# Gating expert results per block and scatter-adding them into an output that already holds the residual rows

## What is computed

```
x  = x + attention(layer_norm(x)) @ Wo + bo
nx = layer_norm(x)
noisy = nx@Wr + br + noise * softplus(nx@Wn + bn)
the two highest of the 8 experts are kept, softmax over the two
out = x                                where sigmoid(nx@Wsk + bsk) > 0.5
out = x + sum over the two e of gate_e * (relu(nx@W1[e] + b1[e]) @ W2[e] + b2[e])   elsewhere
```

## Time and profile before

| | us |
|---|---|
| median of three runs | 861.09 |
| span of the profiled execution, first to last instruction | 859.4 |
| first stage and table, to the first second-stage matmul | about 530 |
| second stage, to the landing of the last scatter | about 238 |
| third stage | about 91.5 |

### The profile page before, as it was taken

One profiled execution on the slowest core, in us unless ns is written; L12 is line 12 of the kernel. 1 busy time (PEld: TensorE's weight loads), 2 busy tenths in 40 slices (PEclk: granted clock), 3 DMA queues, 4 the chain that ended last, 5 costly groups with the idle time before them and its releaser, 6 DMA issues.

```text
span 859.4 us, 32083 instructions
## 1 busy us (share of the span) xinstructions
PE 591.5 (69%) x11076; PEld 428.8 (50%) x11076; DVE 651.0 (76%) x2422; ACT 482.6 (56%) x947; POOL 483.5 (56%) x540
## 2 busy tenths in 40 slices
PE   0668787777778888877776512999999999820000
PEld 0336565555555555555554411777777777610000
DVE  2367888989888888899897571787778877618887
ACT  1547666575756576666665421888888888600000
POOL 3113777777777677777777673266666666530000
PEclk9889799999998789999998555999999999955555
DMA  9862231322213132313435336666777666329997
GB/s 93 253 182 82 59 91 57 90 64 84 87 58 91 52 86 60 92 54 91 105 82 162 101 109 214 255 226 222 238 241 247 224 226 237 117 76 301 292 298 224
DMA packets 164172, 127.32 MB, mean 148 GB/s; under 512 B 38050, under 2 KB 142595, under 8 KB 164128
## 3 DMA queue, kind: packets, MB, share of 16 engines
q1 hardware_dynamic: 127264, 90.00, 35.8%
q10 hardware_dynamic: 24576, 20.98, 8.3%
q0 software_dynamic: 12288, 15.77, 5.6%
HBM read 73.86 MB, written 62.78 MB: 159 GB/s over the span
## 4 chain that ended last, share of the span: by engine, by line
PE 33%; DVE 19%; issue 16%; ACT 14%; DMA 8%; POOL 3%; ACTq 3%; DVEq 2%; SPq 1%; POOLq 0%
DMA out<-z 6%; ACT z L666 5%; PE ps L500 5%; DVE stats L816 4%; PE ps L628 3%; PE ps L616 3%; PE ps L534 3%; PE ps L629 3%; PE ps L630 3%; PE ps L617 3%; PE ps L618 3%; POOL expert_rows L1123 3%; PE ps L537 2%; PE ps L546 2%; ACT hT L695 2%
## 5 line engine op out<-in xcount | busy, mean ns | idle before, releaser
L1123 POOL DMA_INDIRECT expert_rows<-pay,rows_of x256 | 256.7, 1003 | 103.0 <-issue 70.0
L1136 POOL DMA_INDIRECT expert_results<-z,words x128 | 134.5, 1051 | 107.6 <-DVE z L1007 76.3
L1021 DVE TENSOR_TENSOR hlo<-h,hhi 128x512 fp32r<-128x512 f32 x128 | 89.8, 702 | 45.6 <-ACT hhi L773 43.8
L771 ACT ACTIVATE h<-ps,w1x 128x512 f32<-128x512 f32 x128 | 88.2, 689 | 35.2 <-PE ps L618 31.5
L666 ACT ACTIVATE z<-xres,shift,rstd 128x128 f32 (+1 forms) x256 | 102.0, 481 | 2.5 <-DVE shift L848 2.5
L773 ACT ACTIVATE hhi<-ps,w1x 128x512 fp32r<-128x512 f32 x128 | 87.1, 681 | 0.0
L534 PE MATMUL ps<-hT,wq 128*128 128x512 f32 x64 | 47.9, 839 | 55.5 <-ACT hT L695 55.5
L682 ACT ACTIVATE log_var<-var_eps 128x8 f32<-128x8 f32 (+1 forms) x36 | 7.5, 208 | 130.3 <-DVE var_eps L830 110.7
L1104 POOL TENSOR_TENSOR xres<-xres,bo_row 128x512 f32 (+1 forms) x32 | 41.6, 1299 | 55.8 <-ACT z L666 55.5
L546 PEld LDWEIGHTS ps<-pT,v_sb 32*32 32x32 f32 x4096 | 47.6, 106 | 49.0 <-issue 46.8
L546 PE MATMUL ps<-pT,v_sb 32*32 32x32 f32 x4096 | 58.1, 204 | 11.3 <-issue 4.2
(11 more groups left out here) (138 smaller groups left out, 1454.4 us busy)
## 6 DMA issues: line engine op xcount, KB each, us to landing
w1x<-split_weights SPq DMA_DIRECT2D x33, 514.0 KB, 3.7
w2x<-split_weights SPq DMA_DIRECT2D x33, 512.5 KB, 5.0
expert_results<-zeros SPq DMA_DIRECT2D x32, 512.0 KB, 4.1
pay<-expert_rows SPq DMA_DIRECT2D x33, 264.0 KB, 3.5
xres<-in_r_x SPq DMA_DIRECT2D x32, 256.0 KB, 3.1
split_weights<-w2x ACTq DMA_DIRECT2D x16, 512.0 KB
hhi<-expert_results SPq DMA_DIRECT2D x32, 256.0 KB, 3.8
hlo<-expert_results SPq DMA_DIRECT2D x32, 256.0 KB, 3.7
```

What stands on the lines that cost most here:

```text
L771: nc.scalar.activation(h32[:, c % 2], ps[:, c, :], ACT.Relu, bias=b1_c).then_inc(s_h32_made, 1)
L1021: ev.tensor_tensor(hlo[:, c], h32[:, c % 2], hhi[:, c].bitcast(F32), ALU.subtract).then_inc(s_h_lo, 1)
L1123: g.indirect_dma_start(rows, bass.IndirectOffsetOnAxis(ap=rows_of[:, odd, k * J + j:k * J + j + 1], axis=0), pay[:, odd, k, j, :], None, b ...
L1136: g.indirect_dma_start(results, bass.IndirectOffsetOnAxis(ap=words[:, slot, j:j + 1], axis=0), yrow[slot][:, j, :], None, bounds_check=K * ...
```

## The change

- The output tensor gets 512 spare rows behind the 16384 real ones; the host cuts them off. The result table, its zeroing and the whole third stage are gone.
- In the first stage SP stores the finished residual rows x1 of the tile six before the one it loads, 256 KB each (`store_x1`), in the place of zeroing. The last six stores come after the loop and the biases, ahead of the wait for the fill counts. A blank tile is stored to the spare rows.
- `gdiff` is no longer kept. Two DVE instructions write, in columns 129 and 130 of `pay`, the difference v1-v0 for both choices, and v1-v0 or 0 for the numerator. They travel with the row. The wait for the earlier scatter of `pay` comes before them.
- The word is the token's number, the same for both choices. Blank rows have words that point into the spare rows, so that they are written there and no longer dropped.
- In each block ACT makes one `Exp` of the two columns (`gate_rows`), DVE three small instructions (`make_gates`: add one, reciprocal, multiply), and `copy_rows` multiplies by the gate on the way out of PSUM. It also waits for the gate.
- The scatter adds into the output (`compute_op=ALU.add`). Since two blocks can hold the same token, the scatter of a block first waits until all four DMAs of the block before have landed.

The diff, cut to its core (left out: the declarations of buffers and semaphores, and lines that don't change):

```diff
--- before.py
+++ after.py
@@ -53,15 +53,14 @@
+    BEHIND = 4
...
-    out_t = out.rearrange("b t c -> (b t) c").rearrange("(n p) c -> p n c", p=P)
+    out_t = out[0:N, :].rearrange("(n p) c -> p n c", p=P)
...
-    results = nc.dram_tensor("expert_results", [K * N, C], F32, kind="Internal").ap()
-    results_t = results.rearrange("(k n p) c -> p k n c", k=K, p=P)
@@ -187,11 +179,10 @@
-        yin = [hhi[:, 0:K], hhi[:, K:2 * K], hlo[:, 0:K], hlo[:, K:2 * K]]
-        yin = [y.rearrange("p k (j c) -> p k j c", c=C).bitcast(F32) for y in yin]
-        half = z1
-        fin = z2
+        gate_e = sb("gate_e", [P, 4, J, 2])
+        gate_d = sb("gate_d", [P, J])
+        gate_r = sb("gate_r", [P, J])
+        gate = sb("gate", [P, 4, J])
@@ -399,10 +382,10 @@
-            def zero_results(n):
...
-                sp.dma_start(results[bass.ds(n * K * G, K * G), :].rearrange("(p r) c -> p r c", p=P),
-                             zeros[:].unsqueeze(1).to_broadcast([P, K * J, C])).then_inc(s_results_zeroed, 16)
+            def store_x1(n):
...
+                sp.wait_ge(s_x1_made, n + 1)
+                sp.dma_start(out_t[:, bass.ds(n * J, J), :], tiles(xres, n)).then_inc(s_x1_out, 16)
@@ -423,14 +406,13 @@
-            sp.wait_ge(s_zeros_set, 1)
-            with sp.Fori(2, NG - 1, 2) as n:
+            for n in range(2, BEHIND + 2):
+                load_x(n, n % 2)
+            with sp.Fori(BEHIND + 2, NG - 1, 2) as n:
...
-                zero_results(n)
+                store_x1(n - BEHIND - 2)
...
-                zero_results(n + 1)
-            zero_results(0)
-            zero_results(1)
+                store_x1(n - BEHIND - 1)
@@ -449,6 +431,10 @@
+            sp.dma_start(out[N:N + G, :].rearrange("(p j) c -> p j c", j=J),
+                         blank[:, :, 0:C]).then_inc(s_x1_out, 16)
+            for n in range(NG - BEHIND - 2, NG):
+                store_x1(n)
@@ -468,7 +454,8 @@
-                          (s_words_kept, i - 3))
+                          (s_words_kept, i - 3),
+                          (s_gate_exp, i - 3))
@@ -479,18 +466,8 @@
+            apart(sp, (w1_in[0], used * 4 + 16), (w2_in[0], used * 4 + 16))
...
-            def load_results(n, slot):
-                apart(sp, (s_f_made, n - 3))
-                for k in range(K):
-                    sp.dma_start(yin[slot][:, k], results_t[:, k, bass.ds(n * J, J), :]).then_inc(f_in[slot], 16)
...
-            for n in range(4):
-                load_results(n, n)
-            with sp.Fori(4, NG - 3, 4) as n:
-                for d in range(4):
-                    load_results(n + d, d)
@@ -753,9 +730,10 @@
-            act.wait_ge(s_route, NG * ROUTE)
-            nc.scalar.activation(gexp[:], gdiff[:], ACT.Exp).then_inc(s_gate_exp, 1)
...
+            def gate_rows(i, slot):
+                act.wait_ge(e_in[slot], quad(i, slot, 16) + 16)
+                wait(act, s_gate, i - 3)
+                nc.scalar.activation(gate_e[:, slot], xg[slot][:, :, C + 1:C + 3], ACT.Exp).then_inc(s_gate_exp, 1)
@@ -773,20 +751,13 @@
+                    if c == 2:
+                        gate_rows(i + 1, (slot + 1) % 4)
...
+            gate_rows(0, 0)
...
-            def store(n, par):
-                act.wait_ge(s_f_made, n + 1)
-                act.dma_start(out_t[:, bass.ds(n * J, J), :], fin[:, par]).then_inc(f_out[par], 16)
...
-            with nc.scalar.Fori(0, NG - 1, 2) as n:
-                store(n, 0)
-                store(n + 1, 1)
-            for q in f_out:
-                act.wait_ge(q, 16 * NG // 2)
@@ -878,8 +849,11 @@
-                    ev.tensor_tensor(gdiff[:, bass.ds(n * J, J)], top[:, :, 1], top[:, :, 0],
-                                     ALU.subtract).then_inc(s_route, 1)
+                    wait(dve, sent[odd], pair(n, odd, SENT))
+                    second = top[:, :, 1].unsqueeze(1).to_broadcast([P, K, J])
+                    first = top[:, :, 0].unsqueeze(1).to_broadcast([P, K, J])
+                    ev.tensor_tensor(pay[:, odd, 1, :, C + 2], top[:, :, 1], top[:, :, 0], ALU.subtract)
+                    ev.tensor_tensor(pay[:, odd, :, :, C + 1], second, first, ALU.subtract).then_inc(s_route, 1)
@@ -934,6 +908,7 @@
+            dve.wait_ge(s_pay_zeroed, 1)
@@ -976,18 +951,6 @@
-            dve.wait_ge(s_gate_exp, 1)
-            ev.tensor_scalar(gden[:], gexp[:], 1.0, None, ALU.add).then_inc(s_gate, 1)
-            dve.wait_ge(s_gate, 1)
-            ev.reciprocal(gfirst[:], gden[:]).then_inc(s_gate, 1)
-            dve.wait_ge(s_gate, 2)
-            ev.tensor_tensor(gates[:, :, 0], gfirst[:], keep[:], ALU.mult).then_inc(s_gate, 1)
-            ev.tensor_tensor(gsecond[:], gexp[:], gfirst[:], ALU.mult).then_inc(s_gate, 1)
-            dve.wait_ge(s_gate, 4)
-            ev.tensor_tensor(gates[:, :, 1], gsecond[:], keep[:], ALU.mult).then_inc(s_gate, 1)
-            dve.wait_ge(s_gate, 5)
@@ -1004,12 +967,23 @@
-                ev.tensor_copy(yrow[slot].rearrange("p j c -> p (j c)"), ps[:, 6, :]).then_inc(s_yrow_copied, 1)
+                dve.wait_ge(s_gate, i + 1)
+                ev.tensor_tensor(yrow[slot], ps[:, 6, :].rearrange("p (j c) -> p j c", c=C),
+                                 gate[:, slot].unsqueeze(2).to_broadcast([P, J, C]),
+                                 ALU.mult).then_inc(s_yrow_copied, 1)
...
+            def make_gates(i, slot):
+                dve.wait_ge(s_gate_exp, i + 1)
+                ev.tensor_scalar(gate_d[:], gate_e[:, slot, :, 0], 1.0, None, ALU.add).then_inc(s_gate_den, 1)
+                dve.wait_ge(s_gate_den, i + 1)
+                ev.reciprocal(gate_r[:], gate_d[:]).then_inc(s_gate_inv, 1)
+                dve.wait_ge(s_gate_inv, i + 1)
+                ev.tensor_tensor(gate[:, slot], gate_r[:], gate_e[:, slot, :, 1], ALU.mult).then_inc(s_gate, 1)
@@ -1024,34 +998,16 @@
+                make_gates(i + 1, (slot + 1) % 4)
...
+            make_gates(0, 0)
...
-            def combine(n, slot):
-                par = slot % 2
-                dve.wait_ge(f_in[slot], quad(n, slot, 16 * K) + 16 * K)
-                for j in range(J):
-                    m = ev.scalar_tensor_tensor(half[:, par, j:j + 1], yin[slot][:, 0, j:j + 1],
-                                                tile(gates, n, j)[:, 0, 0:1], tile(xres, n, j), ALU.mult, ALU.add)
-                m.then_inc(s_f_half, 1)
-                dve.wait_ge(s_f_half, n + 1)
-                wait(dve, f_out[par], pair(n, par, 16))
-                for j in range(J):
-                    m = ev.scalar_tensor_tensor(fin[:, par, j:j + 1], yin[slot][:, 1, j:j + 1],
-                                                tile(gates, n, j)[:, 0, 1:2], half[:, par, j:j + 1], ALU.mult, ALU.add)
-                m.then_inc(s_f_made, 1)
...
-            for n in range(4):
-                combine(n, n)
-            with nc.vector.Fori(4, NG - 3, 4) as n:
-                for d in range(4):
-                    combine(n + d, d)
@@ -1089,12 +1044,12 @@
-            g.iota(token[:], [[N, K], [P, J]], base=0, channel_multiplier=1,
+            g.iota(token[:], [[0, K], [P, J]], base=0, channel_multiplier=1,
...
-            g.iota(blank_u[:, :, C:C + 1], [[0, J]], base=FAR, channel_multiplier=0).then_inc(s_blank_word, 1)
+            g.iota(blank_u[:, :, C:C + 1], [[1, J]], base=N, channel_multiplier=J).then_inc(s_blank_word, 1)
@@ -1132,17 +1087,19 @@
+                if has(i - 1):
+                    apart(pool, (res_out[(slot - 1) % 4], quad(i - 1, (slot - 1) % 4, 16 * J) + 16 * J))
...
-                    g.indirect_dma_start(results, bass.IndirectOffsetOnAxis(
+                    g.indirect_dma_start(out, bass.IndirectOffsetOnAxis(
...
-                        yrow[slot][:, j, :], None, bounds_check=K * N - 1,
-                        oob_is_err=False).then_inc(res_out[slot], 16)
+                        yrow[slot][:, j, :], None, bounds_check=N + G - 1,
+                        compute_op=ALU.add).then_inc(res_out[slot], 16)
...
-            pool.wait_ge(s_results_zeroed, 16 * NG)
+            pool.wait_ge(s_x1_out, 16 * (NG + 1))
@@ -1165,7 +1122,9 @@
-    out = nc.dram_tensor("out_0", inputs['r_x'].shape, _mybir.dt.float32, kind="ExternalOutput").ap()
+    shape = inputs['r_x'].shape
+    rows = shape[0] * shape[1]
+    out = nc.dram_tensor("out_0", (rows + 512, shape[2]), _mybir.dt.float32, kind="ExternalOutput").ap()
...
-    return r.results[0]["out_0"]
+    return r.results[0]["out_0"][:rows].reshape(shape)

```

More of the change, by code:

```diff
@@ L80, in build @@
         ones = sb("ones", [P, P], BF16)
-        zeros = sb("zeros", [P, P])
         filler = sb("filler", [P, 2 * P], BF16)
@@ L98, in build @@
         noise_sb = sb("noise_sb", [P, N // P, E])
-        gates = sb("gates", [P, N // P, K])
         keep = sb("keep", [P, N // P])
[L101 to L105, removed]
         fill = sb("fill", [P, E])
@@ L267, in build @@
         s_gate_exp = sem("gate_exp")
+        s_gate_den = sem("gate_den")
+        s_gate_inv = sem("gate_inv")
```

(5 more changed lines are left out.)

## The result

The changed kernel takes 926.66 us (median of four runs, 923.2 to 929.68) against 860.84 us for the kernel before: 1.076 times as long, 95% interval 1.0734 to 1.0786. The prediction said 829.7 us and faster. Rivals 2 and 3, each given as a possible cause of a slower run, both came true in part, and together.

What follows compares the result with a forecast made beforehand. PE was taken to pace the second stage, transfers the third. Afterwards the scatter chain binds: S = 4.18 + 3.57 + 0.86 = 8.61 us a block, and 562.7 + 31 S gives 829.7 us, range 780 to 890.

Steps and rivals of the forecast that it cites:

- Rivals 2 and 3: Second stage, together 0.28: 2 (0.18) put POOL's wait for the landing over 4.6 us, slower than before; 3 made issue longer.
- The third stage goes: After the last scatter lands at 767.73 us, the rest of the span, 91.7 us, disappears if nothing else moves.
- The first stage costs nothing: SP's stores of x1 replace zeroing and DVE's added instructions are absorbed: 0 us taken, -2 to +6 kept.
- Gating costs nothing: Second stage: gate multiply, `make_gates` and ACT's exponential are covered by PE's pace: 0 taken, 16 us in all if that fails.
- The scatter becomes a chain of issue, landing and reaction: POOL's new wait in `scatter(i)`: three uncovered terms sum to 8.61 us a block, over 6.71, and bind all engines.
- First to fourth DMA: Chain's issue term in POOL's scatter, from the first DMA's start to the fourth's: 4.18 us a block.
- rival 3: POOL's issue grows, not the landing: 1.5 x 0.97 us per DMA, S 10.6, 890 us; chance 0.28 together with rival 2.
- L = 3.57 us: Chain's landing term, from the fourth DMA's start to its landing, taken from plain scatters beside SP's traffic; ends 2.18 and 6.0.
- Reaction 0.86: Chain's last term, from the landing to POOL's first DMA of the next group: 0.86 us a block.
- POOL's walk through the empty loop: Between blocks 29 and 30 POOL walks through the empty rest of the loop in 12.2 us, covering the wait there.
- The range: 780 to 890 us, leaving out S (chain time a block) under 7.0 (some 0.08) and above 10.6 (some 0.12).
- PE's share of 78%: Sign of being right: PE's busy share in the second stage falls to some 6.7 / 8.6 = 78%.

Runs made afterwards that it cites:

- g1: Changed kernel with gated rows written plainly into a table with a row per token and choice, without wait or sum: 1038.4 us, 0.916 of the kernel before.
- e4: Kernel before plus only the wait for the scatter of the block before, writing plainly to the result table: 1199.5 us, 1.053 of the kernel before.
- e5: Changed kernel, still adding, but POOL waits only where the expert changes: 829.4 us, 0.963 of the kernel before; on another chip 1090.1 us, 0.961.
- e1: Changed kernel with the scatter writing instead of adding, wait kept: 1083.3 us, 0.957 of the kernel before.

## Why the prediction was wrong, step by step

- **The third stage goes, 91.7 us.** Right: 90.5 in the balance.
- **The first stage costs nothing, -2 to +6.** Right: +3.1 in the profiled execution. Among the traces on the usual chips the first scatter comes at 549.3 to 554.0 us with the new first stage, and at 549.9 and 550.6 with the old.
- **Gating costs nothing.** Nearly: 3.8 us (g1).
- **The scatter becomes a chain of issue, landing and reaction, paid 31 times, and all engines fall back to it.** Right, and shown by e4, which has the wait and nothing else, and e5, which keeps the adding and drops most waits.
- **First to fourth DMA, 4.18 us.** This failed. It took the duration of plain DMAs for adding ones and left the difference to rival 3. An adding DMA costs 1.54 us when undisturbed, 0.57 more; rival 3's estimate by counted accesses was 0.49. On average it is 1.71, and the term measured 6.2 us: 2.0 us too small, 63 us over 31 blocks. It was the larger error. Rival 3 added its 0.49 four times; only three issues lie between the starts of the first and the fourth DMA, and the fourth's own issue lies within the landing.
- **L = 3.57 us.** This failed too: 4.75 in the block shown and 4.7 on average, so 1.1 us a block or 34 us. It lay within the ends of 2.18 and 6.0. The row that it came from was right in kind (traffic beside it), but the read was said to have no room beside that contention. It does: 3.4 us alone, and the loads on top.
- **Reaction 0.86.** Right: 0.84.
- **POOL's walk through the empty loop, 12.2 us between blocks 29 and 30.** Wrong: it is 9.8 us (897.25 to 907.03). The 7.3 us that POOL waited there before was for DVE's copy, late since PE and DVE walk through their own empty rest; POOL's walk hides beside the landing. The last steps, with no loads beside them, take 9.7 to 10.7 us in place of 12. So 562.7 + 31 x 11.98 = 934 stands against 928.6 (span and 1.7 us), although the first stage took 3.1 us more. Term by term the account closes: 829.7, plus 63 and 34 for the two sizes, less 4 for the walk and the reaction, plus 3 for the first stage and 2 for the last landing and the end, is 928.
- **The range.** It was cut at S = 10.6 because each rival was costed alone on top of the forecast. With both terms at the values named (4.6 + 0.49 x 4), S is 11.6 and the time 922; with 0.49 three times, 11.1 and 907.
- **PE's share of 78% as a sign of being right.** It was measured as 77%, but by luck. The forecast was 6.7 us of work in 8.6; it became 9.2 us of work in 12.0, as the granted clock fell to 0.81. That fall was not in the prediction.

The Trainium skill's estimate in the prediction (page "DMA: Bandwidth & Descriptors", section "Latency and other measured facts", 0.2 to 2 us per HBM access on top of 2.18) gives 2.4 to 4.2 us: the landing alone, 3.4, lies in it, that beside the loads, 4.75, above it, and the page's rule says nothing on the issue.

## What to carry to other kernels

A wait for a DMA that an engine issues itself turns its issue time, the landing and the reaction into one chain; compare the sum with the pace of the stage, and cost all terms for the new kind of DMA together. Where the wait guards against two writers of one row, wait only at the blocks that can hold the same row; here that is 7 of 31, and on one chip it turned 69 us lost into 31 us won. A landing is no constant: a plain one took 2.2 to 2.4 us in e1 where a 1 MB load was issued a microsecond or more behind it, and 4.0 to 5.7 where the load came nearer or ahead.

## What the runs showed of the hardware

- An indirect DMA of 128 rows of 512 bytes keeps POOL 0.97 us when it writes and 1.54 us when it adds. Its packets change as well: before, the software queue had 12288 packets for 384 DMAs, 32 each; after, it has 26624, and with 32 for each of the 256 in the first stage that leaves 144 for each adding DMA, about one per row. The queue's share of the engines' time rose from 5.6% to 12.2% for nearly the same bytes. Its row before:

```profile
q0 software_dynamic: 12288, 15.77, 5.6%
```

- Without other traffic the add lands in 3.36 us from its start, the write in 2.2.
- Some of POOL's DMA instructions take longer, and why isn't shown. The two at 649.32 and 651.57 took 1.95 and 2.06 us, the one at 663.23 took 1.81. DVE was at work beside them, among other things on a cast between two SBUF tiles, which itself took 0.52 us in the first block and 0.42 in the next:

```profile
650.97 0.52 DVE L957 CAST xhi<-x 128x512 fp32r<-128x512 f32 x1
...
663.54 0.42 DVE L957 CAST xhi<-x 128x512 fp32r<-128x512 f32 x1
```

The Trainium skill's page "SBUF — State Buffer", section "Who interferes with whom", says that a cast can enter DVE's 2-port mode, and that in it whichever of DVE and GpSimd issues first blocks the other for the whole instruction. The casts lie within or at the end of the instructions at 663.23 and 649.32, and may be a part of their excess of 0.3 and 0.4 us over 1.54. The longest, at 651.57, starts after the cast has ended at 651.49, so a cast does not explain it, and no run here does.
